# A grouped convolution on TensorE: from full-array matmuls of eight positions to four 64x64 tiles of four positions

## What is computed

```python
x = x + attn(cond(x, cond_128, ...))     # mixing, 32-head causal attention with an adapter prefix, projection
x = x + ffn(cond2(x, cond_128, ...))     # the convolution, then the expert layer

def cond2(x, c, weight, c_weight, bias):  # x (32, 64, 1024); weight (64, 16, 9); GROUPS = 4, PAD = 4
    out = lax.conv_general_dilated(x, weight, window_strides=(1,), padding=[(4, 4)],
                                   dimension_numbers=('NCH', 'OIH', 'NCH'), feature_group_count=4)
    return out + (c @ c_weight.T)[:, :, None] + bias[None, :, None]

def ffn(x, ...):                          # 2048 tokens of 1024
    base = xf @ W_base.T + b_base         # plus a router over 8 experts, top 2, and rank-16 adapters
    return base + lora
```

## Time and profile before

| | us |
|---|---|
| median of 3 runs | 1141.3 |
| the runs | 1140.57, 1141.3, 1144.7 |
| span of the profiled execution, first to last instruction | 1139.1 |
| TensorE busy (records overlap) | 1132.2 |
| VectorE busy | 923.4 |
| ScalarE busy | 359.6 |
| GpSimd busy | 54.1 |

### The profile page before, as it was taken

One profiled execution on the slowest core, in us unless ns is written; L12 is line 12 of the kernel. 1 busy time (PEld: TensorE's weight loads), 2 busy tenths in 40 slices (PEclk: granted clock), 3 DMA queues, 4 the chain that ended last, 5 costly groups with the idle time before them and its releaser, 6 DMA issues.

```text
span 1139.1 us, 21477 instructions
## 1 busy us (share of the span) xinstructions
PE 1132.2 (99%) x8632; PEld 950.7 (83%) x8632; DVE 923.4 (81%) x1740; ACT 359.6 (32%) x665; POOL 54.1 (5%) x24
## 2 busy tenths in 40 slices
PE   9999999999999999999999999999999999999998
PEld 6888888888888888888888888878888888888887
DVE  5999879879889789798798799888767777877765
ACT  5433333333342432433433334323222211122210
POOL 0000000000000000000000000110000022221112
PEclk9999999999999999999999999999999999999999
DMA  6515115114125034034033177885549933233312
GB/s 222 182 56 167 67 34 162 66 53 153 56 75 167 20 97 155 12 106 146 20 111 130 45 270 269 322 251 164 185 129 347 345 89 104 96 116 116 98 38 93
DMA packets 99701, 151.81 MB, mean 133 GB/s; under 512 B 7443, under 2 KB 84115, under 8 KB 96915
## 3 DMA queue, kind: packets, MB, share of 16 engines
q1 hardware_dynamic: 98594, 135.76, 36.5%
q10 hardware_dynamic: 1008, 14.68, 3.1%
HBM read 95.88 MB, written 54.54 MB: 132 GB/s over the span
## 4 chain that ended last, share of the span: by engine, by line
PE 92%; DVE 4%; DMA 2%; issue 1%; ACT 0%; SPq 0%; DVEq 0%; ACTq 0%
PE psum L948 44%; PE psum L1026 23%; PE psum L1044 5%; PE psum L931 3%; PE psum L916 2%; PE psum L900 2%; PE psum L1078 2%; PE psum L1060 2%; PE psum L276 2%; DMA y_scratch<-a_ysb 2%; PE psum L960 2%; PE psum L909 1%; PE psum L1062 1%; PE psum L972 1%; PE psum L230 1%
## 5 line engine op out<-in xcount | busy, mean ns | idle before, releaser
L948 PE MATMUL psum<-z,w_hi 128*128 128x512 f32 x1536 | 481.5, 395 | 0.2 <-DVE z L374 0.2
L948 PEld LDWEIGHTS psum<-z,w_hi 128*128 128x128 f32 x1536 | 282.5, 188 | 57.2 <-DVE z L374 0.4
L948 PE MATMUL psum<-z,w_lo 128*128 128x512 f32 x768 | 300.5, 391 | 0.0
L1026 PE MATMUL psum<-f_wform,f_act_hi 128*128 128x512 f32 (+1 forms) x912 | 279.9, 389 | 1.3 <-DVE f_u L1494 1.1
L1026 PEld LDWEIGHTS psum<-f_wform,f_act_hi 128*128 128x128 f32 x912 | 167.9, 188 | 35.8 <-issue 2.6
L1026 PE MATMUL psum<-f_wform,f_act_lo 128*128 128x512 f32 (+1 forms) x456 | 176.2, 386 | 0.0
L948 PEld LDWEIGHTS psum<-z,w_lo 128*128 128x128 f32 x768 | 144.1, 188 | 30.6
L1026 PEld LDWEIGHTS psum<-f_wform,f_act_lo 128*128 128x128 f32 x456 | 85.7, 188 | 17.4
L875 POOL TENSOR_TENSOR f_xn<-f_x,_bbase 128x1024 f32<-128x1024 f32 x16 | 50.5, 3158 | 1009.0 <-DVE f_x L1520 678.5
L1218 ACT ACTIVATE f_act_hi<-f_act_sum 128x512 fp32r<-128x512 f32 x64 | 40.3, 632 | 119.2 <-DVE f_act_sum L1469 48.1
L1218 ACT ACTIVATE f_act_hi<-f_raw 128x512 fp32r<-128x512 f32 x56 | 33.7, 626 | 102.7 <-DVE f_raw L1552 64.8
(11 more groups left out here) (173 smaller groups left out, 1491.7 us busy)
## 6 DMA issues: line engine op xcount, KB each, us to landing
w_forms<-f_prep_lo SPq DMA_DIRECT2D x16, 896.0 KB, 5.2
f_wform<-w_forms SPq DMA_DIRECT2D x7, 2048.0 KB, 13.2
f_wform<-w_forms ACTq DMA_DIRECT2D x7, 2048.0 KB, 16.9
w_st<-in_wqkvT SPq DMA_DIRECT2D x7, 1536.0 KB, 6.3
w_forms<-f_prep_hi SPq DMA_DIRECT2D x16, 640.0 KB, 6.2
m_x<-in_x SPq DMA_DIRECT2D x16, 512.0 KB, 5.5
y_scratch<-a_ysb SPq DMA_DIRECT2D x32, 256.0 KB, 2.8
f_raw<-y_scratch SPq DMA_DIRECT2D x8, 1024.0 KB, 6.0
```

The lines of the kernel that those rows point to most:

```text
L948: mm = pe.matmul(dst, w[:, c, x, :], zs, start=(c == 0 and i == 0), stop=(c == KC - 1 and i == 2))
L1026: mm = pe.matmul((prod_bank[i], bank[0])[part][:, cols], a[:, c, :], wform[i][:, w, c, cols], start=(i < 4 and c == 0 and n == 0), stop=(c ...
```

## The change

The block of positions becomes four, so that an output block needs three input blocks, and the batch moves from the free axis into the partitions:

- a partition is now (batch, position in a block of four, channel): 64 partitions for each batch. Blocks are kept in two sets, by whether their number is even or odd (`e`, `side`), so the free axes of `x8` are group, side and m.
- `toep` is [128, 4, 3, 64], the same for the two batches.
- `convolve` does 4 groups x 2 parities x 3 blocks x 2 batches x 2 halves of m = 96 matmuls of 64 x 64 x 64. The batch chooses the half of the array's rows and the PSUM bank, the half of m chooses the half of the output partitions; the result has the layout that it had. Both batches' signals come with the last matmuls.
- `spread` issues 16 transfers of 16 partitions by 4 groups by 128, where it issued 8 of 16 by 8 by 128. The bytes are the same.
- the cleared edges are one column of each of two sides over all partitions.

```diff
+NTAP = 3
+PW = PH // 2
+XW = L // PH + 2
-        toep = both.take("toep", [P, CONV, 2, P])
+        toep = both.take("toep", [P, CONV, NTAP, NC])
-        x8 = both.take("x8", [P, 2 * CONV, L // PH + 1])
+        both.take("aggT_rest", [P, CONV * (2 * P - NTAP * NC)])
+        x8 = both.take("x8", [P, CONV, 2, XW])
...
-                for f in range(PH):
-                    q, u = (f - TAPS // 2) % PH, int(f < TAPS // 2)
-                    sp.dma_start(x8[p % 2][CG * f:CG * (f + 1), :, u:u + L // PH],
-                                 x1_dram[p].rearrange("(g c) (q m) -> c g q m", c=CG, q=PH)[:, :, q, :]
-                                 ).then_inc(x8_in[p % 2], 16)
+                src = x1_dram[p].rearrange("(b g c) (e f m) -> b f c g e m", b=2, c=CG, e=2, f=PW)
+                for b in range(2):
+                    for f in range(PW):
+                        at0 = NC * b + CG * f
+                        for e in range(2):
+                            sp.dma_start(x8[p % 2][at0:at0 + CG, :, e, 1:1 + L // PH], src[b, f, :, :, e, :]
+                                         ).then_inc(x8_in[p % 2], 16)
...
-                pe.wait_ge(x8_in[p % 2], 16 * PH * (p // 2 + 1))
+                pe.wait_ge(x8_in[p % 2], 16 * 2 * PH * (p // 2 + 1))
                 wait(pe, conv_set, 2 * p if p >= 2 else 0)
-                for b in range(2):
-                    for g in range(CONV):
-                        for j in range(2):
-                            o = 512 * b + P * g
-                            mm = pe.matmul(conv_banks(p)[:, o:o + P], x8[p % 2][:, CONV * b + g, j:j + P], toep[:, g, j, :],
-                                           start=(j == 0), stop=(j == 1))
-                    mm.then_inc(conv_mm, 1)
+                for g in range(CONV):
+                    for e in range(2):
+                        for j in range(NTAP):
+                            side, shift = (e + j - 1) % 2, (e + j - 1) // 2
+                            for b in range(2):
+                                rows = slice(NC * b, NC * (b + 1))
+                                for half in range(2):
+                                    o, m0 = 512 * b + P * g + NC * e, 1 + shift + NC * half
+                                    mm = pe.matmul(conv_banks(p)[NC * half:NC * (half + 1), o:o + NC],
+                                                   x8[p % 2][rows, g, side, m0:m0 + NC], toep[rows, g, j, :],
+                                                   start=(j == 0), stop=(j == NTAP - 1))
+                                if g == CONV - 1 and e == 1 and j == NTAP - 1:
+                                    mm.then_inc(conv_mm, 1)
...
-                    dve.memset(x8[0][0:P // 2, :, 0:1], 0.0).then_inc(edges, 1)
-                    dve.memset(x8[0][P // 2:P, :, L // PH:L // PH + 1], 0.0).then_inc(edges, 1)
+                    dve.memset(x8[0][:, :, 1, 0:1], 0.0).then_inc(edges, 1)
+                    dve.memset(x8[0][:, :, 0, XW - 1:XW], 0.0).then_inc(edges, 1)
```

More of the change, by code:

```diff
@@ L478, in program @@
         wh_both = at("wh_both", wh.manual_sbuf_range[0], [P, KC, 2, HIDDEN], F32R)
-        x8 = [x8, sb("x8_next", [P, 2 * CONV, L // PH + 1])]
+        x8 = [x8, sb("x8_next", [P, CONV, 2, XW])]
         ctxb = [sb(f"ctxb{t}", [P, P]) for t in range(2)]
@@ L1735, in group @@
                     dve.wait_ge(y_copied, NG * NU)
-                    dve.memset(x8[1][0:P // 2, :, 0:1], 0.0).then_inc(edges, 1)
-                    dve.memset(x8[1][P // 2:P, :, L // PH:L // PH + 1], 0.0).then_inc(edges, 1)
+                    dve.memset(x8[1][:, :, 1, 0:1], 0.0).then_inc(edges, 1)
+                    dve.memset(x8[1][:, :, 0, XW - 1:XW], 0.0).then_inc(edges, 1)
                 if G == 2:
@@ L1801, in layouts @@
     w = v["L0_cond2_weight"]
-    toep = np.zeros((P, CONV, 2, P), np.float32)
+    toep = np.zeros((P, CONV, NTAP, NC), np.float32)
     for g in range(CONV):
[L1805 to L1808, removed]
+        for j in range(NTAP):
+            for f in range(PW):
+                for q in range(PW):
+                    tap = PW * j + f - q
                     if 0 <= tap < TAPS:
-                        toep[f * CG:(f + 1) * CG, g, j, q * CG:(q + 1) * CG] = w[g * CG:(g + 1) * CG, :, tap].T
+                        for b in range(2):
+                            toep[NC * b + f * CG:NC * b + (f + 1) * CG, g, j, q * CG:(q + 1) * CG] = w[g * CG:(g + 1) * CG, :, tap].T
     last = np.concatenate([v["L0_ffn_W_base"], v["L0_ffn_A"].reshape(NE * RANK, L), v["L0_ffn_W_router"]], 0)
```

## The result

The changed kernel takes 1178.34 us (median of 5 runs, 1177.21 to 1185.36) where the kernel before takes 1141.3: a ratio of 1.0337, 95% interval 1.032 to 1.0354, 37 us slower. The forecast was 1134.1 with a range up to 1144. The profiled execution has a span of 1179.4 us against 1139.1.

The account below looks back on a forecast made before the run. TensorE was taken as the bound, with 92% of the chain. 16 convolutions at 0.45 us saved give 7.2 us less, other terms nothing: span 1139.1 to 1131.9, plus 2.2 around it, 1134.1 us; range 1129 to 1144.

Parts of the forecast that it names:

- The tiles' pace: Convolution on TensorE: four 64x64 tiles run side by side, 2.75 us first to last record instead of 3.46.
- Entry: Start of each convolution on TensorE: changing the tiling makes the first record come 0.32 us after the preceding one.
- refilling of the array: End of each convolution on TensorE: an estimated 0.04 us more, added to the exit cost.
- The rival in which the row halves do not overlap: Convolution's row tiles run one after the other: 6.02 us against 3.46, +41 us, so 1182; chance 0.10.
- a floor of 25 ns a record: Convolution on TensorE: every record costs at least 25 ns, 4.8 us for 192, time 1167; chance 0.04.
- Issue is no limit: Convolution on TensorE: 192 records need one each 15 ns, and the engine can take one every 11.4 ns.
- The rival of stalls in a long run of short records: Convolution on TensorE: each further 32 records cost 0.14 us extra, +0.70 a convolution; 1145, half of it 1139.7; chance 0.17.
- 16 cost 5.9 to 7.4 us ... I take 6.3: SyncE's queue: issuing the 16 transfers of a set takes 6.3 us, where eight took 3.69.
- Cost on the path: nothing: SyncE's longer sets delay store, reload and VectorE, but cover absorbs it; without cover up to 2.6 us in six groups.
- The rival of SyncE's loop: SyncE, reload, GpSimd, VectorE: a round of 32.8 us exceeds TensorE's 32.3, 0.5 us in six groups, 1137; chance 0.09.
- GpSimd's addition and the router: VectorE's router, even with both shifted additions falling on it whole, ends before TensorE wants its result.
- The fit by 0.3 us: VectorE's router ends at 1057.6 and TensorE wants its result at 1057.86.
- The evacuation at the end: VectorE evacuates both halves, some 1.3 us, after the convolution; the following product leaves 1.4 us of cover.

Follow-up runs that it names:

- e3: Changed kernel with one tile of 64 rows by 128 columns in place of two of 64 by 64 (192 instructions per convolution): 1176.57 us.
- e14: e11 with the spread of position 3 issued earlier, ahead of a load that SyncE has to wait for: 1132.81 us, ratio 0.9923.
- e1: Kernel before, old convolution, with only the eight transfers of a spread cut into sixteen of 64 pieces: 1159.43 us against 1141.75.
- e8: e1 with SyncE's stores and reloads issued between the spreads and position 3's spread moved behind the two writings back: 1155.4 us against 1141.04.
- e10: Changed kernel with stores and reloads between the spreads on SyncE and 256 instructions per convolution in place of 384: 1147.15 us against 1141.04.
- e11: e10 with two loads of router constants ahead of position 3's spread and the accumulation flag only at a group's first matmul: 1144.6 us against 1140.86.

## Why the prediction was wrong, point by point

**The tiles' pace held.** An undisturbed convolution takes 2.81 us from first to last record, where 2.75 was taken and 2.82 worked out first: 58.5 ns for four records of 64 columns, all four tiles side by side. Entry 0.32 and exit 0.15 were forecast as 0.32 and 0.16; between the same neighbours that makes 3.28 us in place of 3.72, a saving of 0.445. The product behind it takes 0.02 more; for this refilling of the array the prediction had an estimate of 0.04 with no row behind it. That leaves 0.425 saved, where 0.45 was taken. (A slip without effect: counted like L931, the 16 records of L972 give 0.69/7.5 = 92 ns a matmul, not 86.) The rival in which the row halves do not overlap did not come about (it did in e3, with wider tiles), nor did a floor of 25 ns a record; the page "TensorEngine Tiling (Array Packing)" of the Trainium skill, section "Performance Considerations", gives about 60 cycles a matmul. By the estimate of 25 ns that the prediction made from it, 14.7 ns a record contradict it if it is meant for the whole engine.

**"Issue is no limit" failed.** The step took the 11.4 ns a record of L900's block of 64 records as a rate that TensorE keeps up. That block has 128 instructions (5.6 ns each); the convolution has 384 in 2.81 us, 7.3 ns each, but three times as many in a row. The profiles' pages give the size of a packet of instructions: 2560 matmul records more, thus 5120 instructions, came with 20 more packets (89, and 69 in the kernel before); in e14 3072 more came with 12. So 256 instructions to a packet, which is also the grid of the stalls. At 7.3 ns one is used up in 1.87 us; with 256 instructions in 2.64 us, none stalls. In the trace nine of the ten stalls end 2.2 to 2.9 us after the start of such a packet (itself 0.9 to 1.4 us long), the tenth 3.2 (1.8 long). That the next packet is not there within those 1.9 us fits all of it; what decides when it is asked for no run shows. The rival of stalls in a long run of short records had the right place, priced by another mechanism: +0.70 us a convolution, where 1.5 came (23.7/16).

**"16 cost 5.9 to 7.4 us ... I take 6.3" failed.** Undisturbed they cost 7.40 to 7.42: a transfer of 64 pieces holds SyncE as long as one of 128, 0.47 us from start to start. The interpolation from a transfer of one piece was wrong, the upper bound right. Beside that, single transfers took 1.2 to 2.0 us, one to three in a group; in the changed kernel's expert groups each of these began within 0.3 us of a packet of instructions. That is a coincidence in time, and not the whole story: in e14 six such transfers of 1.2 to 1.4 us, one in each group, lie 7.7 us and more from any packet. No run took the packets away from SyncE's transfers.

**"Cost on the path: nothing" failed with it.** The step followed one group in which TensorE sets the pace. It found VectorE 0.3 us late, at most 2.6, and set that to nothing because of the cover. Its own figure without cover, 2.6 us in each of six groups, is 15.6 us in all; it stands in none of the cases and outside the range. e1 lost 17.7.

**Its rival had the mechanism, and one term wrong.** The rival of SyncE's loop put a set at the upper bound already (32 transfers at 0.46 and two contexts are its 15.6), so the price of a transfer isn't what it missed; it still made a round 32.8 us where e1's take 35.4. Term by term against e1's round from 970.28 to 1006.34, which is 36.06: two sets with contexts 16.7 for 15.6; store to reload 2.8 for 2.7; on to the next store 0.4 as said; from there to the reload 5.6 for 3.5; landing 3.4 for 3.3; addition 3.0 for 3.1; VectorE's step and evacuation 4.1 for 4.2. The largest miss is the second store. The rival let it start 0.4 us behind the first reload, but took its 3.5 us from a row in which it started 1.2 behind the earlier trace rows. With 0.4 it takes 4.9 to 5.6 us in all six rounds of e1, and so it did in the one such case of the kernel before (SyncE's queue there):

```profile
912.15 0.34 SPq L715 DMA_DIRECT2D f_x<-x_scratch  x1
912.53 0.43 SPq L793 DMA_DIRECT2D out<-f_x  x1
917.58 0.32 SPq L715 DMA_DIRECT2D f_x<-x_scratch  x1
```

The reload waits for the store, so 917.58 is when it has landed, 5.05 us after its issue. That the first reload, under way beside it, is the reason is likely but not shown: one store of the kernel before took 5.6 us with 1.15 between (at 1078.07). Most of the rest is single long transfers inside the sets. The rival priced the mechanism at 3 us (1137 against 1134.1), with a margin of 0.5 us in a round, and gave it a chance of 0.09.

**GpSimd's addition and the router held:** no wait for the router stands in TensorE's waits, neither in the changed kernel nor in e14. The fit by 0.3 us itself was not put to the test: the changed kernel's rounds are 37 us long, and e14 has another order on SyncE. **The evacuation at the end held:** in e14 no wait for it.

**The writing back was not weighed.** The working followed SyncE's queue in the last full group only. At the turn to the experts the same longer set puts a writing back behind the first weight transfers: 21.75 us to land, 5.7 us on the path.

## What to carry to other kernels

Price a change that splits transfers by their number, not their pieces. Sum every loop that passes through the issuing queue, and take each term from a row in which the transfers stand as close together as they will after the change: a landing read from a row with more room was most of what this sum lacked. Where a loop comes within a few per cent of the bounding engine's round, move the stores and reloads ahead of bulk transfers that nobody waits for yet. When matmuls get smaller, count instructions per microsecond over the whole block, and join those that share a stationary tile before anything else: here 256 in 2.6 us ran without a stall and 384 in 2.8 us did not. A stall that keeps its place in the instruction stream while everything around it moves points at the supply of instructions. And when a repair brings less than expected, look for a second cause that hides behind the first, round by round: e8's time said "no effect" while five of its six rounds were fully repaired.

## What the runs showed of the hardware that was not expected

- TensorE ran 256 instructions in 2.64 us without a stall (e10, e14) and stalled for 1.2 to 3.6 us in 10 of 16 convolutions with 384 in 2.81 us. The stalls lie whole multiples of 256 instructions apart.
- Four tiles of 64x64 overlapped fully (58.5 ns for four records of 64 columns), while two tiles of 64 rows by 128 columns did not overlap at all (55.8 ns each, e3).
- A transfer holds SyncE 0.47 us with 64 pieces and with 128; while weights were read through another queue, single ones held it 3.7 to 5.0 us (e11) and a load of 64 KB took 36 us to land (e8). In the same stretch of the kernel before such loads held it 0.32 us and landed after 10.6 and 12.3 us, so the weights alone don't do it; what else must be under way no run shows.
- A store of 512 KB issued 0.4 us behind a reload of 512 KB took 4.9 to 5.6 us to land (e1, six times); issued 1.2 us behind, 3.5 in three of four cases (kernel before).
- After a pause of 10.4 us TensorE was granted 0.61 of its clock over the next 5.5 us, which cost another 2.1 us.
